# Three stretches of a causal attention reordered: the first queries' rotation, the output weights' split, the third norm's first transposes

## The chip, the cores and the metric

The kernel runs on one core of a Trainium2 chip. The metric is the device time of one execution in microseconds (us); lower is better. All positions below are counted from the start of the profiled execution's span.

## The reference

One layer over 512 rows of width 1024: x = x + cross_attention(norm(x)), x = x + causal_attention(norm(x)), x = x + feed_forward(norm(x)). The change touches the second part and the step into the third:

```python
q = x @ Wq + x @ q_A @ q_B          # 16 heads of 64; k and v have 4 heads
q, k = _rms_norm(q), _rms_norm(k)
q, k = _apply_rope(q, cos, sin), _apply_rope(k, cos, sin)
q = q * q_gain
attn = softmax(where(causal, q @ k.T * scale, -inf))
y = attn @ v
vn = v / maximum(sqrt(sum(v * v)), 1e-12)
y_out = y - sum(y * vn) * vn
out = y_out @ Wproj + y_out @ p_A @ p_B
x = x + out                          # then layernorm, router, experts
```

The feed-forward part has 16 routed experts (two for each row) and a shared one.

## The kernel before

Every large product is made in three passes of split operands (`matmul_3pass`, L32 to L34: hi by hi, hi by lo, lo by hi). The Scalar Engine (ACT) makes the hi half of an operand with a copy, VectorE (DVE) the lo half with a subtraction. Each engine has its own instruction list, written out by hand, and goes through it in order; semaphores join the lists. There is no planner, so the order in the source is the order in the queues.

`attention` holds both attentions. The cross attention (64 steps) ends near 900 us. Then the projections of the causal attention are made in twelve pieces, `ORDER`: four pieces hold keys and values of a block of 128 rows, eight hold half of a block's queries. Seven pieces (`AHEAD`) are made before the heads, and the other five are filled in between them.

For a piece, ACT copies the product out (`copy_piece`) and squares it by heads (`square_piece`), GpSimd (POOL) turns the mean squares into a factor (`root`, L651 and L654) and multiplies by the sines (`turn_by_sin`, L663), DVE multiplies by the factor (L1302) and by the cosines (L1305) in `turn_by_cos` and adds both parts in `rotate` (L1322). TensorE (PE) transposes the result (`turn_piece`, L846) and ACT copies it to `c_kT` or `c_qT` (`turned_piece`, L1097). Piece 4 is the first piece of queries. `unit_values` (L1330, L1332) squares and sums the values, POOL takes the square root (L711), and `unit_values_2` makes the unit vectors `vn`.

The heads go in 32 units of two heads, one a step, in 34 steps `st`. In each step PE makes the scores of unit st (L888), transposes the probabilities of unit st - 1 (L901) and multiplies those of unit st - 2 with the values (L917); DVE makes the maxima (`maxima`, L1347 and L1351), copies half of the transposed probabilities (`pt_dve`) and scales the result (`take_y`, L1369); ACT copies the other half (`pt_act`, L1104) and makes the exponentials (`exps`, L1113). Between these, PE does a third of a projection piece in each step (`fill`), from step 16 on a third of an output tile. `slot` places the transposes of query pieces and of finished rows (`turn_y`, L928; ACT `xt_hi`, L1060; DVE `xt_lo`, L1290) at half steps. POOL and DVE take the part along the value out of y: `times_value` (L681), `dot` (L1376), `part_along` (L687), `take_along` (L1383).

The weights of the output come as four pieces of 1 MB, w = 6 to 9, into two raw buffers. `weights_hi` (ACT, L1032) and `weights_lo` (DVE, L1222) split them in steps 10 to 18; the next load into a buffer waits for the split of the piece before it. After the steps PE makes the last transposes of rows (`turn_y`, 14 and 15), the transposes of the third norm's rows (`turn_xn`, L996) and output tiles 6 and 7 (`output`). `third_norm` (DVE, L96) makes those rows. Output tile 6 needs `xt_lo` of the last rows. The causal attention and this step end near 1128 us.

Of the kernel before, what the change touches and what calls it, by code (L numbers as in the profile page):

```python
# [427 lines left out]
def attention(nc, m, ins, resid, QT, K, V, raw, s_sb, PT, at, kv_loaded, ident, y_dram, ln, d, F, weff, weff_stored):  # L428
# [18 lines left out]
    with ExitStack() as stage:  # L447
# [60 lines left out]
        def w_piece(x, w):  # L508
            return x[:, (w // 2) % 2, 4 * (w % 2):4 * (w % 2) + 4, :]

        def w_raw(w):
            return raw[:, w % 2, :].rearrange("p (e n) -> p e n", n=W)
# [72 lines left out]
        with nc.Block() as block:  # L585
# [38 lines left out]
            def _(pool):  # L624
# [23 lines left out]
                def root(i):  # L648
                    n = heads(i)
                    pool.wait_ge(s["piece_out"], i + 1)  # L650
                    pool.tensor_scalar(ms[:, i % 3, 0:n], ms[:, i % 3, 0:n], 1.0 / HD, RMS_EPS,  # L651
                                       ALU.mult, ALU.add).then_inc(s["ms_done"], 1)
                    pool.wait_ge(s["ms_done"], i + 1)
                    pool.tensor_tensor(ms[:, i % 3, 0:n], ms[:, i % 3, 0:n],  # L654
                                       consts[:, 1:2].to_broadcast([P, n]), ALU.pow).then_inc(s["rms_done"], 1)

                def turn_by_sin(i):
                    n = heads(i)
                    pool.wait_ge(s["normed"], i + 1)
                    if i >= 2:  # L660
                        pool.wait_ge(s["rotated"], i - 1)
                    for k in range(2):
                        pool.tensor_tensor(half(sq[:, i % 2, :], i, k), half(piece_row(i), i, 1 - k),  # L663
                                           sin[:, tile_of(i), :].unsqueeze(1).to_broadcast([P, n, 32]),
                                           ALU.mult).then_inc(s["sin_done"], 1)
# [40 lines left out]
                for i in range(1, 5):  # L706
                    root(i)
                    turn_by_sin(i - 1)
                turn_by_sin(4)
                pool.wait_ge(s["vss"], 1)  # L710
                pool.tensor_tensor(vss[:, :], vss[:, :], consts[:, 2:3].to_broadcast([P, TB * HKV]),  # L711
                                   ALU.pow).then_inc(s["vnorm"], 1)
                root(5)
                turn_by_sin(5)
                root(6)
                turn_by_sin(6)
# [21 lines left out]
            def _(pe):  # L738
# [249 lines left out]
                def turn_xn(t):  # L988
                    pe.wait_ge(ln.xn_done, 2 * TB + t + 1)
                    for h in range(2):  # L990
                        n = 2 * t + h
                        if n >= 4:
                            pe.wait_ge(d["xt_lo_done"], n - 3)
                        for i in range(4):
                            e = 4 * h + i
                            mm = pe.transpose(xn_bank(n)[:, i * P:(i + 1) * P], F["xn"][:, t, e * P:(e + 1) * P],  # L996
                                              ident[:, :])
                        mm.then_inc(d["xt_ready"], 1)

                pe.wait_ge(s["y_done"], UNITS)  # L1000
                turn_y(4 * TB - 2)
                turn_y(4 * TB - 1)
                turn_xn(0)
                turn_xn(1)
                output(6, 0, DB)
                turn_xn(2)
# [7 lines left out]
            def _(act):  # L1014
# [11 lines left out]
                def weights_hi(w):  # L1026
                    raw_loaded(act, w % 2, w // 2 + (w >= 2))
                    if w < 4:
                        act.wait_ge(b["scores_ready"], STEPS if w >= 2 else SPLITS)
                    else:  # L1030
                        act.wait_ge(s["group_done"], w // 2 - 1)
                    act.activation(w_piece(K_hi, w), w_raw(w), ACT.Copy).then_inc(s["w_hi"], 1)  # L1032

                def step(base, u, known):
                    qb = u % TB
# [114 lines left out]
                for st in range(UNITS + 2):  # L1150
                    if st in TAKEN:
                        copy_piece(AHEAD + TAKEN.index(st))
                    slot(2 * st)
                    if 1 <= st <= UNITS:
                        pt_act(st - 1)
                    if st < UNITS:
                        exps(st)
                    if st == 0:
                        square_piece(6)
                    if st in TAKEN:  # L1160
                        square_piece(AHEAD + TAKEN.index(st))
                    slot(2 * st + 1)
                    for w, turn in ((6, 10), (7, 11), (8, 16), (9, 17)):
                        if st == turn:
                            weights_hi(w)

                def xn_hi(n):
                    act.wait_ge(d["xt_ready"], n + 1)
# [23 lines left out]
            def _(dve):  # L1192
# [27 lines left out]
                def weights_lo(w):  # L1220
                    dve.wait_ge(s["w_hi"], w + 1)
                    dve.tensor_tensor(w_piece(K_lo, w), w_raw(w), f32(w_piece(K_hi, w)),  # L1222
                                      ALU.subtract).then_inc(s["w_split"], 1)

                def add_x(t):

# [83 lines left out]
                def rotate(i):  # L1310
                    n = heads(i)
                    dve.wait_ge(s["cos_done"], i + 1)
                    dve.wait_ge(s["sin_done"], 2 * i + 2)
                    for k, op in enumerate((ALU.add, ALU.subtract)):
                        out = piece_row(i)
                        in0, in1 = half(cosp[:, i % 2, :], i, k), half(sq[:, i % 2, :], i, k)
                        if i < TB:
                            out = out.rearrange("p (h c d) -> p h c d", h=n, c=2)[:, :, :, k * 32:(k + 1) * 32]
                            in0, in1 = (x.unsqueeze(2).to_broadcast([P, n, 2, 32]) for x in (in0, in1))
                        else:  # L1320
                            out = out.rearrange("p (h d) -> p h d", d=HD)[:, :, k * 32:(k + 1) * 32]
                        ins_ = dve.tensor_tensor(out, in0, in1, op)  # L1322
                    ins_.then_inc(s["rotated"], 1)
# [4 lines left out]
                def unit_values():  # L1328
                    dve.wait_ge(s["piece_out"], TB)
                    dve.tensor_tensor(v_sq[:, :], v_flat, v_flat, ALU.mult).then_inc(s["v_step"], 1)  # L1330
                    dve.wait_ge(s["v_step"], 1)
                    dve.tensor_reduce(vss[:, :], v3(v_sq[:, :]), AX.X, ALU.add).then_inc(s["vss"], 1)  # L1332
# [66 lines left out]
                def third_norm(t):  # L1399
                    if t == 0:  # L1400
                        dve.wait_ge(s["w_split"], 10)
                    ln.norm(dve, 2, resid, F["xn"], mean_var, rstd, t)
# [43 lines left out]
                for i in range(1, 5):  # L1446
                    turn_by_cos(i)
                    rotate(i - 1)
                unit_values()
                rotate(4)  # L1450

                def slot(k):
                    for n, at_slot in ROWS_SLOTS.items():
# [3 lines left out]
                for st in range(UNITS + 2):  # L1457
                    if st >= 19 and st % 3 == 1:
                        add_out((st - 19) // 3)
                    slot(2 * st)  # L1460
                    if st < UNITS:
                        maxima(st)
                    if 1 <= st <= UNITS:
                        pt_dve(st - 1)
                        row_recip(st - 1)
                    if st >= 2:
                        take_y(st - 2)
                    if st >= 4 and st % 2 == 0:
                        dot((st - 4) // 2)
                    if st >= 5 and st % 2 == 1:  # L1470
                        take_along((st - 5) // 2)
                    slot(2 * st + 1)
                    if st == 0:
                        turn_by_cos(5)
                    if st == 1:
                        rotate(5)
                        unit_values_2()
                    if st == 2:
                        turn_by_cos(6)
                    if st == 3:  # L1480
                        rotate(6)
                    if st - 1 in TAKEN:
                        turn_by_cos(AHEAD + TAKEN.index(st - 1))
                    if st - 2 in TAKEN:
                        rotate(AHEAD + TAKEN.index(st - 2))
                    for w, turn in ((6, 10), (7, 12), (8, 16), (9, 18)):
                        if st == turn:
                            weights_lo(w)
                    if st >= 20 and st % 3 == 2:
                        half_stats((st - 20) // 6, (st - 20) // 3 % 2)  # L1490
                    if st in (27, 33):
                        third_norm((st - 27) // 6)
                dot(15)
                take_along(15)
                add_out(5)
                xt_lo(4 * TB - 2)
                xt_lo(4 * TB - 1)
# [1047 lines left out]
```

## Time and profile before

| | |
|---|---|
| runs of the kernel | 1451.96, 1452.84, 1455.63 us (median 1452.84) |
| profiled execution, its own time | 1451.73 us |
| its span | 1450.1 us |
| PE busy (matmuls) | 1408.3 us, 97% of the span |
| DVE busy | 845.6 us, 58% |
| ACT busy | 530.3 us, 37% |
| POOL busy | 202.8 us, 14% |
| median from issue to landing of a load of output weights | 4.7 us |

A row of the timeline has the start, the duration (from the first start to the last end, for several instructions in one row), engine, line and operation, the tiles written and read, and the count; in brackets stands the idle time before it and what ended it. The granted clock is that of TensorE, 1.00 for 2.4 GHz and 0.50 for 1.2 GHz. Matmul durations overlap each other, so the distance of two starts says more than one duration.

### The profile page before, as it was taken

Reading aid. Unit: us, or ns where it says so; the run is one execution under the profiler, and the core shown is the slowest. Engines: PE = TensorE matmul, PEld = TensorE weight load, DVE = VectorE, ACT = ScalarE, POOL = GpSimd, SP = SyncE. Lnnn points to the kernel's source line nnn. Section 1 sums busy time; section 2 is a strip of 40 time slices with the busy share of each in tenths; the row PEclk is TensorE's granted clock in tenths of the full one; section 3 lists DMA queues with packets and bytes.
Section 4 is the critical chain, followed back from the end, with each engine's and each line's share of the span. In section 5 each row is a group of like instructions: output and inputs, shape, how many; then the busy total and the mean of one; then the engine's idle time right before and its main releaser. Section 6 shows DMA issues by size and latency. Waiting matters only on the chain. (4 is left out here: it accounts for less than half of the span.)

```text
span 1450.1 us, 18196 instructions
## 1 busy us (share of the span) xinstructions
PE 1408.3 (97%) x6676; PEld 1151.2 (79%) x6676; DVE 845.6 (58%) x1232; ACT 530.3 (37%) x947; POOL 202.8 (14%) x264
## 2 busy tenths in 40 slices
PE   7999999999999999999999999899999899998998
PEld 5878788888888888888888888776778788887786
DVE  5554455555555455455554557678765676676655
ACT  3222322332223322223222223556432435665561
POOL 3000100000000000000000000455311022122132
PEclk9999999999999999999999999999999999999999
DMA  7453643333333333333333322201100566886766
GB/s 251 152 202 118 247 176 118 116 109 108 123 123 111 113 108 115 131 108 116 108 112 131 108 98 77 107 1 59 34 1 1 175 210 228 299 294 222 266 224 218
DMA packets 43487, 203.64 MB, mean 140 GB/s; under 512 B 5233, under 2 KB 5297, under 8 KB 31985
## 3 DMA queue, kind: packets, MB, share of 16 engines
q1 hardware_dynamic: 30016, 152.32, 30.1%
q0 software_dynamic: 9568, 36.35, 7.7%
q10 hardware_dynamic: 3840, 14.16, 2.5%
q8 instruction: 37, 0.61, 0.2%
q14 instruction: 26, 0.20, 0.0%
HBM read 182.36 MB, written 20.45 MB: 140 GB/s over the span
## 5 line engine op out<-in xcount | busy, mean ns | idle before, releaser
L32 PE MATMUL banks<-V_hi,b_PT_hi 128*128 128x512 f32 x512 | 205.6, 401 | 0.0
L1024 ACT ACTIVATE b_PT_hi<-banks 128x512 fp32r<-128x512 f32 x64 | 38.3, 599 | 446.9 <-PE banks L757 446.9
L32 PE MATMUL banks<-K_hi,QT_hi 128*128 128x512 f32 x512 | 199.3, 389 | 2.5 <-PEq L157 2.5
L34 PE MATMUL banks<-V_hi,b_PT_lo 128*128 128x512 f32 x512 | 200.2, 391 | 0.0
L33 PE MATMUL banks<-V_lo,b_PT_hi 128*128 128x512 f32 x512 | 199.6, 390 | 0.0
L34 PE MATMUL banks<-K_hi,QT_lo 128*128 128x512 f32 x512 | 199.4, 389 | 0.0
L33 PE MATMUL banks<-K_lo,QT_hi 128*128 128x512 f32 x512 | 199.2, 389 | 0.0
L1247 DVE TENSOR_TENSOR b_scores<-banks,b_scores 128x512 f32<-128x512 f32 x64 | 44.2, 691 | 202.0 <-PE banks L34 202.0
L642 POOL DMA_DIRECT2D b_scores<-mask x60 | 32.2, 537 | 639.2 <-PE banks L757 621.4
L2176 DVE TENSOR_TENSOR e_lo<-e_raw,e_hi 128x1024 fp32r<-128x1024 f32 x80 | 95.2, 1231 | 38.4 <-ACT e_hi L2012 37.3
L32 PEld LDWEIGHTS banks<-K_hi,QT_hi 128*128 128x128 f32 x512 | 96.1, 188 | 22.8 <-issue 2.9
L34 PEld LDWEIGHTS banks<-V_hi,b_PT_lo 128*128 128x128 f32 x512 | 96.1, 188 | 21.0
L34 PEld LDWEIGHTS banks<-K_hi,QT_lo 128*128 128x128 f32 x512 | 96.1, 188 | 20.0
L33 PEld LDWEIGHTS banks<-K_lo,QT_hi 128*128 128x128 f32 x512 | 96.1, 188 | 19.9
L33 PEld LDWEIGHTS banks<-V_lo,b_PT_hi 128*128 128x128 f32 x512 | 96.4, 188 | 18.5
L32 PEld LDWEIGHTS banks<-V_hi,b_PT_hi 128*128 128x128 f32 x512 | 96.2, 188 | 18.0
L1267 DVE TENSOR_TENSOR V_lo<-raw,V_hi 128x2048 fp32r<-128x2048 f32 x30 | 68.8, 2292 | 64.4 <-ACT V_hi L1048 64.4
L1267 DVE TENSOR_TENSOR K_lo<-raw,K_hi 128x2048 fp32r<-128x2048 f32 x30 | 68.8, 2293 | 61.8 <-ACT K_hi L1048 61.8
L2012 ACT ACTIVATE e_hi<-e_raw 128x1024 fp32r<-128x1024 f32 x80 | 81.4, 1060 | 23.0 <-DMA e_raw<-w_down 16.1
L1204 DVE SCALAR_TENSOR_TENSOR resid<-resid,b_alpha,banks 128x1024 f32<-128x1024 f32 x60 | 76.5, 1275 | 6.8 <-PE banks L34 6.8
L32 PE MATMUL banks<-K_hi,V_hi 128*128 128x512 f32 x160 | 68.2, 427 | 0.8 <-ACT c_piece L1069 0.8
L34 PE MATMUL banks<-K_hi,V_lo 128*128 128x512 f32 x160 | 64.0, 400 | 0.0
(327 smaller groups left out, 2752.4 us busy)
## 6 DMA issues: line engine op xcount, KB each, us to landing
raw<-kv SPq DMA_DIRECT2D x60, 1024.0 KB, 4.7
e_raw<-w_up SPq DMA_DIRECT2D x40, 512.0 KB, 5.0
e_raw<-w_down SPq DMA_DIRECT2D x40, 512.0 KB, 5.9
b_scores<-mask POOLq DMA_DIRECT2D x64, 256.0 KB, 2.9
d_s_raw<-shared_w SPq DMA_DIRECT2D x32, 512.0 KB, 4.9
raw<-xattn_w SPq DMA_DIRECT2D x11, 1024.0 KB, 4.9
y_dram<-c_zeros ACTq DMA_DIRECT2D x1, 6656.0 KB, 28.0
raw<-attn_w SPq DMA_DIRECT2D x6, 1024.0 KB, 4.7
```

What stands on the lines that cost most here:

```text
L32: pe.matmul(out, lhs_hi, rhs_hi, start=first, stop=False)
L33: pe.matmul(out, lhs_hi, rhs_lo, start=False, stop=False)
L34: return pe.matmul(out, lhs_lo, rhs_hi, start=False, stop=last)
L642: pool.dma_start(s_sb[:, u, :], ins["mask"][it * 4 + u]).then_inc(mask_loaded[u], 16)
L1024: act.activation(PT_hi[:, u % 2, :], T_ps[:, u % 2, :], ACT.Copy).then_inc(b["pt_hi"], 1)
L1204: op = dve.scalar_tensor_tensor(resid[:, qb, :], resid[:, qb, :], alpha[:, qb:qb + 1], O_ps(u), ALU.mult, ALU.add)
L1247: dve.tensor_tensor(s_sb[:, u % 4, :], S_ps[:, u % 2, :], s_sb[:, u % 4, :], ALU.add).then_inc(b["masked"], 1)
L1267: dve.tensor_tensor(split_tile(False, u), raw_tile(u), f32(split_tile(True, u)), ALU.subtract).then_inc(b["kv_split"], 1)
L2012: act.activation(e_hi[:, first + j, :], e_raw[:, j, :], ACT.Copy).then_inc(s["e_hi"], 1)
L2176: dve.tensor_tensor(e_lo[:, first + j, :], e_raw[:, j, :], f32(e_hi[:, first + j, :]), ALU.subtract).then_inc(s["e_split"], 1)
```

## The change

Three edits. First, DVE rotates piece 4 before `unit_values()`, and POOL takes `root(5)` before the root of the values' squares. Second, each of the output weight pieces is split in two halves of 128 x 1024, one a step, on ACT in steps 10 to 13 and 15 to 18 and on DVE in steps 11 to 14 and 16 to 19. Third, PE transposes the third norm's first rows (`turn_xn(0)`) before the last rows of heads, and DVE makes the norm of rows 1 after the last `take_along` and not in step 33.

```diff
--- before.py
+++ after.py
@@ -707,10 +707,10 @@
                     root(i)
                     turn_by_sin(i - 1)
                 turn_by_sin(4)
+                root(5)
                 pool.wait_ge(s["vss"], 1)
                 pool.tensor_tensor(vss[:, :], vss[:, :], consts[:, 2:3].to_broadcast([P, TB * HKV]),
                                    ALU.pow).then_inc(s["vnorm"], 1)
-                root(5)
                 turn_by_sin(5)
                 root(6)
                 turn_by_sin(6)
@@ -997,10 +997,10 @@
                                               ident[:, :])
                         mm.then_inc(d["xt_ready"], 1)
 
+                turn_xn(0)
                 pe.wait_ge(s["y_done"], UNITS)
                 turn_y(4 * TB - 2)
                 turn_y(4 * TB - 1)
-                turn_xn(0)
                 turn_xn(1)
                 output(6, 0, DB)
                 turn_xn(2)
@@ -1030,6 +1030,15 @@
                     else:
                         act.wait_ge(s["group_done"], w // 2 - 1)
                     act.activation(w_piece(K_hi, w), w_raw(w), ACT.Copy).then_inc(s["w_hi"], 1)
+
+                def output_weights_hi(w, part):
+
+                    if part == 0:
+                        raw_loaded(act, w % 2, w // 2 + 1)
+                        act.wait_ge(s["group_done"], w // 2 - 1)
+                    rows = slice(2 * part, 2 * part + 2)
+                    act.activation(w_piece(K_hi, w)[:, rows, :], w_raw(w)[:, rows, :],
+                                   ACT.Copy).then_inc(s["w_hi"], 1)
 
                 def step(base, u, known):
                     qb = u % TB
@@ -1160,9 +1169,9 @@
                     if st in TAKEN:
                         square_piece(AHEAD + TAKEN.index(st))
                     slot(2 * st + 1)
-                    for w, turn in ((6, 10), (7, 11), (8, 16), (9, 17)):
-                        if st == turn:
-                            weights_hi(w)
+                    for w, turn in ((6, 10), (7, 12), (8, 15), (9, 17)):
+                        if turn <= st < turn + 2:
+                            output_weights_hi(w, st - turn)
 
                 def xn_hi(n):
                     act.wait_ge(d["xt_ready"], n + 1)
@@ -1221,6 +1230,14 @@
                     dve.wait_ge(s["w_hi"], w + 1)
                     dve.tensor_tensor(w_piece(K_lo, w), w_raw(w), f32(w_piece(K_hi, w)),
                                       ALU.subtract).then_inc(s["w_split"], 1)
+
+                def output_weights_lo(w, part):
+                    rows = slice(2 * part, 2 * part + 2)
+                    dve.wait_ge(s["w_hi"], 2 * w - 6 + part + 1)
+                    op = dve.tensor_tensor(w_piece(K_lo, w)[:, rows, :], w_raw(w)[:, rows, :],
+                                           f32(w_piece(K_hi, w))[:, rows, :], ALU.subtract)
+                    if part:
+                        op.then_inc(s["w_split"], 1)
 
                 def add_x(t):
 
@@ -1446,8 +1463,8 @@
                 for i in range(1, 5):
                     turn_by_cos(i)
                     rotate(i - 1)
+                rotate(4)
                 unit_values()
-                rotate(4)
 
                 def slot(k):
                     for n, at_slot in ROWS_SLOTS.items():
@@ -1483,15 +1500,16 @@
                         turn_by_cos(AHEAD + TAKEN.index(st - 1))
                     if st - 2 in TAKEN:
                         rotate(AHEAD + TAKEN.index(st - 2))
-                    for w, turn in ((6, 10), (7, 12), (8, 16), (9, 18)):
-                        if st == turn:
-                            weights_lo(w)
+                    for w, turn in ((6, 11), (7, 13), (8, 16), (9, 18)):
+                        if turn <= st < turn + 2:
+                            output_weights_lo(w, st - turn)
                     if st >= 20 and st % 3 == 2:
                         half_stats((st - 20) // 6, (st - 20) // 3 % 2)
-                    if st in (27, 33):
-                        third_norm((st - 27) // 6)
+                    if st == 27:
+                        third_norm(0)
                 dot(15)
                 take_along(15)
+                third_norm(1)
                 add_out(5)
                 xt_lo(4 * TB - 2)
                 xt_lo(4 * TB - 1)
```

## Rows read from the trace of the kernel before

**Rows 1.** windows of 50 us: PE, PEld, DVE, ACT, POOL busy, clock, DMA
```profile
900.00:950.00 50.00, 45.97 (x206) 36.39 (x205) 32.84 (x48) 26.32 (x110) 22.60 (x27) 0.93 0.30 106
```

**Rows 2.** windows of 1 us, PE: length, busy, granted clock, DMA share, GB/s
```profile
990.00:991.00 1.00, 0.24 (x3) 0.96 0.50 205
...
994.00:995.00 1.00, 1.00 (x7) 0.83 0.35 49
```

**Rows 3.** PE's waits from 980 to 1025: us in total, times, longest
```profile
PE banks L901 <- ACT c_probs L1113: 1.2, 2, 0.8
PE banks L917 <- ACT c_qT L1097: 0.8, 1, 0.8
PE banks L32 <- ACT c_piece L1069: 0.8, 1, 0.8
PE banks L917 <- DVE V_lo L1290: 0.6, 2, 0.3
```

**Rows 4.** timeline, DVE, 920 to 962: start, us, line, tiles, count, idle before
```profile
936.45 1.21 DVE L1330 TENSOR_TENSOR c_v_sq<-c_v 128x1024 f32<-128x1024 f32 x1
...
938.83 0.77 DVE L1322 TENSOR_TENSOR c_piece<-c_cosp,c_sq 128x256 f32<-128x256 f32 x2
...
948.02 0.74 DVE L1322 TENSOR_TENSOR c_piece<-c_cosp,c_sq 128x256 f32<-128x256 f32 x2
...
951.38 0.27 DVE L1369 TENSOR_TENSOR c_y<-banks,c_recip 128x128 f32<-128x128 f32 x1
```

**Rows 5.** timeline, POOL, 920 to 962
```profile
934.13 2.11 POOL L663 TENSOR_TENSOR c_sq<-c_piece,c_sin 128x256 f32<-128x256 f32 x2 [0.63 <-DVE c_piece L1302]
938.99 3.00 POOL L711 TENSOR_TENSOR c_vss<-c_vss,c_consts 128x16 f32<-128x16 f32 x1 [2.75 <-DVE c_vss L1332]
...
942.37 1.63 POOL L654 TENSOR_TENSOR c_ms<-c_ms,c_consts 128x8 f32<-128x8 f32 x1
945.01 1.92 POOL L663 TENSOR_TENSOR c_sq<-c_piece,c_sin 128x256 f32<-128x256 f32 x2 [1.01 <-DVE c_piece L1302]
```

**Rows 6.** timeline, PE, 925 to 965
```profile
939.65 1.09 PE L846 MATMUL banks<-ident,c_piece 128*128 128x128 f32 x4 [2.42 <-DVE c_piece L1322]
941.43 0.80 PE L888 MATMUL banks<-c_kT,c_qT 64*128 64x128 f32 x4 [0.69 <-ACT c_qT L1097]
```

**Rows 7.** timeline, ACT, 920 to 962
```profile
937.77 0.59 ACT L1069 ACTIVATE c_piece<-banks 128x512 f32<-128x512 f32 x1
```

**Rows 8.** timelines of DVE, POOL and PE, 975 to 1030
```profile
983.75 2.82 DVE L1222 TENSOR_TENSOR K_lo<-raw,K_hi 128x2048 fp32r<-128x2048 f32 x1
...
983.18 3.98 POOL L663 TENSOR_TENSOR c_sq<-c_piece,c_sin 128x256 f32<-128x256 f32 x2 [0.63 <-DVE c_piece L1302]
...
995.27 0.70 PE L888 MATMUL banks<-c_kT,c_qT 64*128 64x256 f32 x4
```

**Rows 9.** groups by form, 900 to 1130: busy us, mean ns, idle before
```profile
L1411 DVE TENSOR_TENSOR d_s_lo<-d_s_raw,d_s_hi 128x1024 fp32r<-128x1024 f32 x2 | 2.4, 1217 | 0.0
```

**Rows 10.** timeline, PE, 1086 to 1135
```profile
1105.62 1.06 PE L928 MATMUL banks<-ident,c_y 128*128 128x128 f32 x8 [1.99 <-DVE c_y L1383]
1106.52 3.17 PE L996 MATMUL banks<-ident,e_raw 128*128 128x128 f32 x16
1109.34 0.77 PE L32 MATMUL banks<-K_hi,V_hi 128*128 128x512 f32 x1
...
1110.34 0.42 PE L34 MATMUL banks<-K_hi,V_lo 128*128 128x512 f32 x1
```

**Rows 11.** timelines of DVE and POOL, 1086 to 1135
```profile
1102.77 1.23 DVE L96 TENSOR_SCALAR e_raw<-resid,c_mean_var,c_rstd 128x1024 f32<-128x1024 f32 x1
1103.92 0.41 DVE L1376 TENSOR_REDUCE c_dots<-c_along 128x4 f32<-128x256 f32 x1
...
1111.31 0.81 DVE L96 TENSOR_SCALAR e_raw<-resid,c_mean_var,c_rstd 128x1024 f32<-128x1024 f32 x1
...
1102.60 0.85 POOL L681 TENSOR_TENSOR c_along<-c_y,c_vn 128x256 f32<-128x256 f32 x1 [2.93 <-DVE c_y L1369]
```

## The prediction

> **What bounds the kernel now.** I read the page first. TensorE (PE) is busy 97% of the span, so a change can only pay where PE waits or where its clock falls. The windows of 50 us show where that is: in 900 to 950, where the causal attention begins, PE is busy 46.0 us and its granted clock is 0.93 [rows 1]. The windows of 1 us show what a fall costs. The clock was 0.96 of full in 990 to 991, 0.50 in the three windows after it, and 0.83 in 994 to 995 [rows 2]: it fell from the 2.4 GHz to the 1.2 GHz level for 0.08 + 3 + 0.34 = 3.4 us, right after PE had waited twice for 0.8 us [rows 3]. At half speed that is 1.7 us lost, the price I use for one fall below. Then the chain of waits and the timeline give the three places the diff touches. I count times in the old trace from the span's start, and take three savings A, B and C.
>
> **A, the first queries' rotation.** VectorE (DVE) begins `unit_values()`, the squares of the values and their sums, at 936.45 and comes to `rotate(4)` at 938.8 [rows 4]. PE waits for exactly this: its transposes `turn_piece(4)` start at 939.65 after 2.42 us of idleness, and the first scores at 941.43, after 0.69 us more [rows 6]. New order: `rotate(4)` runs 936.5 to 937.2, its sines being ready at 934.1 + 2.1 = 936.2 [rows 5]. `turn_piece(4)` follows `turn_piece(3)` without a gap, at 937.3. Scalar Engine (ACT) must then copy the result to `c_qT`, but its copy of piece 6 stands ahead and ends at 938.3 [rows 7]; the copy of about 0.6 us ends at 938.9. So the first scores move from 941.4 to 938.9, 2.5 us.
>
> What is late next? The values' squares are now behind the rotation, so they end at 939.6 instead of 938.8, and GpSimd (POOL) takes its root of them (3.0 us) from 939.7 to 942.7. It does `root(5)` first, which costs 1.9 us (its longer instruction 1.63) [rows 5] but falls into time in which POOL idled for 2.7 us. Before, the sines of piece 5 stood behind both roots and started at 945.0; now they start at 942.7 and end at 944.6. `rotate(5)` then runs at 944.7 instead of 948.0, 3.3 us earlier [rows 4]; it was queued behind the second maxima, which come early enough now. Behind it, in DVE's order, stand `unit_values_2()`, the third maxima and `take_y(0)`, which ended at 951.65 [rows 4] and now end at 948.3. PE's `turn_piece(5)` waits for that. So A is worth 3.3 us by then. PE, at full clock, would be there 1.8 us before it and waits. If the low clock of before comes back (the first scores took 0.80 us in it [rows 6]), some 3 us remain all the same, since PE then arrives late and DVE's chain is hidden. Low bound 1.5 (the wait of 1.8 us brings one fall behind it), high bound 4.3 (DVE not in the way). The number of instructions doesn't change.
>
> The Trainium skill (SBUF — State Buffer, section Who interferes with whom) says that VectorE operations with two SBUF inputs and GpSimd operations exclude each other for a whole instruction. The trace agrees in part: a subtraction took 2.82 us where POOL's pair of multiplications took 3.98 at the same time [rows 8]. By that rule the squares would wait for `root(5)` until 938.2 and A would be 2.3 instead of 3.3.
>
> **B, the output weights by halves.** Before, DVE subtracts a whole weight piece at the end of step 10: it starts at 983.75 and takes 2.82 us, so the maxima of step 11, ready earlier, come late; ACT's exponentials come late, and PE's transposes wait 0.8 us for them. ACT then converts a whole weight piece of its own before the copy of piece 10, and PE waits 0.8 us for that copy [rows 3, 8]. These two waits and the fall that followed are 0.8 + 0.8 + 1.7 = 3.3 us. In the new order step 10 has no DVE half, and steps 11 and 12 have one each. A half is about 1.22 us on DVE, by the row of the same subtraction at that size [rows 9]; two are 2.44 where one whole beside POOL took 2.82 [rows 8], so the split itself costs some tenths of a us in all, on engines with slack in the other steps. I followed DVE: maxima(11) at 983.9, the half ends about 988.6, maxima(12) ends at 989.7 and its exponentials at 990.7. PE comes for them at 992.6. So the scores of step 13 start at 992.0 instead of 995.27 [rows 8], which is 3.3 us.
>
> Then it gives a part back. In steps 13 and 14 the halves meet the cosines and the rotation of piece 10. DVE has about 5.3 us of work in each, and PE 4.1 to 4.9. The rows of heads, `xt_lo(8)` and `xt_lo(9)`, come 0.2 us later each than PE, and the waits for them (0.6 in all [rows 3]) grow to 1.0. A half on ACT at the end of step 15 delays nothing that PE waits for: the copy of piece 10's transposes, for which PE waits 0.8 us [rows 3], stands ahead of it. In step 18 PE's last transposes of a piece wait about 0.9 us for `take_y`, as maxima(18) stand behind a half. The wait of 0.4 us in step 17 for the exponentials goes, as before it stood behind a whole subtraction. Net 3.3 - 0.4 + 0.4 - 0.5 = 2.8 us. Bounds 0.5 (a fall in steps 15 to 17, with 0.6 lost to longer waits) and 3.7. The loads are no matter: a raw buffer is free one or two steps later, and its 1 MB lands 4.7 us after the issue, with over 4 us left before the step that reads it.
>
> **C, the third norm.** Before, PE has nothing from 1103.6 until its transposes at 1105.62, 1.99 us [rows 10]: `take_along(15)` waits for POOL, which waits for `dot(15)` at 1103.92, and that stood behind a norm of 1.23 us [rows 11]. New: `turn_xn(0)` fills PE at 1103.6 with 0.8 us of transposes (16 took 3.17 us at half clock, so 8 take 0.8 [rows 10]). `dot(15)` needs POOL's product, which was there at 1102.60 + 0.85 = 1103.45 [rows 11], so the chain is 0.4 us earlier and `turn_y` starts at 1105.2 and ends at 1106.0. The norm of row 1 runs 1105.0 to 1105.8, since POOL is idle then (0.81 us in that state, 1.23 beside POOL [rows 11]). `turn_xn(1)` ends at 1106.8. `add_out(5)` (0.7) and `xt_lo(14)` (0.7) follow the norm and end at 1107.1, which releases output(6). It started at 1109.34, and its first two products ran at the low clock, so that the third began at 1110.34 where it now begins at 1107.64 [rows 10]. C is 2.7 us. If the clock falls all the same, it is 1.0; if the norm takes 1.23, it is 2.3. Everything behind output(6) hangs on it, up to the end of the block at 1128.
>
> **Sum.** 3.3 + 2.8 + 2.7 = 8.8 us with no new fall. PE's idle stretches are shorter but not gone. The wait of 1.8 us at 946.5 and two of about 0.8 in steps 15 and 16 look like those after which the clock fell. I take half of one fall, 0.8 us: 8.0 us. The profiled execution took 1451.73 (span 1450.1), which gives 1443.7; the median of the runs is 1.1 above it, so 1444.8.
>
> **Rivals.**
> - *The waits move and the clock falls in the new ones* (0.26). For it speaks that PE then waits on DVE in the steps named. With two or three falls the gain is 8.8 - 3.4 to 8.8 - 5.1, so 1447.5 to 1449. Against: the wait of 0.8 us for `c_qT` [rows 3] had no fall behind it. The Trainium skill (TensorE: Matmul & The Clock Gate, section The HAM clock gate) says that the gate judges by a free-running measure, so that the same wait may or may not be followed by a fall; the trace agrees, since waits of 0.8 us went both ways.
> - *The time is taken back* (0.10). The feed-forward part streams expert weights, and where loads set its pace an earlier start might not end earlier. Against: those loads are issued only after routing, which follows output(7), so they move along. Two thirds lost would give 1449 to 1452.
> - *DVE becomes the bound and keeps PE at 1.2 GHz* (0.04). One mechanism: the halves in steps 13 to 19 stall PE in each step and the clock stays low through all of them. Those are some 30 us, of which half, 15 us, would be added, less the 6 of A and C: 1462. It decides from about 9 us of low clock net of B on. Against: before, the waits of steps 13 to 17 with whole pieces had no fall.
> - *More than forecast* (0.08): a fall elsewhere goes, or A reaches its high bound: 1441 to 1442.
> - *The forecast*, all three waits gone with at most one fall: gain 7 to 9.5, 1443.3 to 1446 (0.52).
>
> **The numbers.** Faster and slower are counted from 0.3% (4.4 us), about what a measurement here can tell. Faster: the forecast, the better case, and two thirds of the first rival, 0.77, of which I keep 0.76 as the runs of before spread over 3.7 us. Slower is the third rival, 0.04; no change the rest, 0.20. Eight in ten: 1441.5 to 1450.
>
> **What would show it.** A: no idle over 1 us before `turn_piece(4)`, first scores near 938.9, a new wait near 946.5. B: step 13's scores 3.3 us earlier against step 10's, at full clock. C: `turn_xn(0)` right behind the last output block and output(6) 2.2 us earlier against it. I am wrong if the squares or `take_y(0)` come later than worked out, or if the clock is 0.50 in more stretches than before.

## The result, and the profile after

The changed kernel takes 1447.79 us (median of 16 runs, 1444.25 to 1452.07) against 1452.86 us of before (16 runs). The ratio (time over that of before) is 0.9965, with a 95% interval of 0.9955 to 0.9974: 5.1 us or 0.35% faster, between 3.8 and 6.5. The forecast was 8.0 us. The time lies in its range, and its direction was right; the size was 1.6 times too large. The profiled execution's span is 1447.4 us.

First edit. PE's timeline of the changed kernel, from 936 us (start, duration, line, tiles, count, idle time before and what ended it):

```profile
939.07 0.66 PE L846 MATMUL banks<-ident,c_piece 128*128 128x128 f32 x4 [0.30 <-DVE c_piece L1339]
940.43 0.49 PE L888 MATMUL banks<-c_kT,c_qT 64*128 64x128 f32 x4 [0.70 <-ACT c_qT L1106]
...
950.00 0.66 PE L846 MATMUL banks<-ident,c_piece 128*128 128x128 f32 x4 [0.43 <-DVE c_y L1386]
```

DVE and POOL in the same stretch of the same kernel:

```profile
938.24 0.78 DVE L1339 TENSOR_TENSOR c_piece<-c_cosp,c_sq 128x256 f32<-128x256 f32 x2 [0.18 <-issue]
938.94 1.21 DVE L1347 TENSOR_TENSOR c_v_sq<-c_v 128x1024 f32<-128x1024 f32 x1
...
949.68 0.27 DVE L1386 TENSOR_TENSOR c_y<-banks,c_recip 128x128 f32<-128x128 f32 x1
```

```profile
938.20 1.63 POOL L654 TENSOR_TENSOR c_ms<-c_ms,c_consts 128x8 f32<-128x8 f32 x1
941.49 2.89 POOL L712 TENSOR_TENSOR c_vss<-c_vss,c_consts 128x16 f32<-128x16 f32 x1 [1.65 <-DVE c_vss L1349]
944.34 1.41 POOL L663 TENSOR_TENSOR c_sq<-c_piece,c_sin 128x256 f32<-128x256 f32 x2
```

This execution entered the causal attention 1.53 us later than that of before (its first key transposes stand at 929.55, those of before at 928.02), for a reason outside the change: its clock was at half level for one stretch from 156 to 159.4 us, behind an idle 2.50 us of PE that the profile of before has too. Eight of this study's 14 profiles have that stretch, and their first key transposes stand at 929.2 to 929.8; in the six without it they stand at 927.4 to 928.6. So places are compared against the first key transposes. The idle 2.42 us of [rows 6] is now 0.30, and the first scores stand 10.88 us behind the first key transposes instead of 13.41.

Second edit. PE, DVE and POOL at steps 13 and 14, and the windows of 1 us behind them (length, PE busy, granted clock, DMA share, GB/s):

```profile
990.19 0.70 PE L888 MATMUL banks<-c_kT,c_qT 64*128 64x256 f32 x4
...
995.00 0.70 PE L888 MATMUL banks<-c_kT,c_qT 64*128 64x256 f32 x4
...
997.67 1.08 PE L917 MATMUL banks<-c_v,c_PT 128*128 128x64 f32 x8 [1.37 <-DVE V_lo L1307]
```

```profile
995.17 1.75 DVE L1237 TENSOR_TENSOR K_lo<-raw,K_hi 128x1024 fp32r<-128x1024 f32 x1
996.84 0.68 DVE L1307 TENSOR_TENSOR V_lo<-banks,V_hi 128x512 fp32r<-128x512 f32 x1
```

```profile
994.61 2.89 POOL L663 TENSOR_TENSOR c_sq<-c_piece,c_sin 128x256 f32<-128x256 f32 x2 [0.83 <-DVE c_piece L1319]
```

```profile
998.00:999.00 1.00, 1.00 (x9) 1.00 0.00 0
999.00:1000.00 1.00, 1.00 (x4) 0.50 0.00 0
...
1002.00:1003.00 1.00, 1.00 (x8) 0.80 0.61 90
```

The two waits of 0.8 us of [rows 3], for the probabilities of step 11 and the copy of piece 10, are gone: step 13 stands 13.06 us behind step 10, before 16.45. But in step 14 PE waits 1.37 us for `xt_lo(8)`, which stands on DVE behind a half that took 1.75 us beside POOL's sines, and then the clock goes to 1.2 GHz for 3.4 us. Step 15 comes 12.41 us behind step 13, before 9.56.

Third edit. PE and DVE at the end of the steps:

```profile
1101.27 1.04 PE L996 MATMUL banks<-ident,e_raw 128*128 128x128 f32 x8
1103.00 1.06 PE L928 MATMUL banks<-ident,c_y 128*128 128x128 f32 x8 [0.70 <-DVE c_y L1400]
1103.90 1.04 PE L996 MATMUL banks<-ident,e_raw 128*128 128x128 f32 x8
1105.04 0.50 PE L32 MATMUL banks<-K_hi,V_hi 128*128 128x512 f32 x1
```

```profile
1102.43 0.42 DVE L1400 TENSOR_TENSOR c_y<-c_y,c_along 128x256 f32<-128x256 f32 x1 [0.73 <-POOL c_along L687]
1102.77 0.81 DVE L96 TENSOR_SCALAR e_raw<-resid,c_mean_var,c_rstd 128x1024 f32<-128x1024 f32 x1
```

`turn_xn(0)` fills PE, 0.70 us of the 1.99 us of idleness [rows 10] remains, the norm takes 0.81 us, and output(6) starts 17.55 us behind step 31, before 19.65.

The table takes differences of PE's start times in the timelines: first key transposes (k), scores of steps 3, 10, 13, 15, 20 and 31, first product of output(6), first product after the attention (e), end of the span. It is for all profiles of this study.

```
kernel            k to 3  3-10  10-13  13-15  15-20  20-31  31-out6  out6-e  e-end
before             25.43  25.37  16.45   9.56  25.05  59.81   19.65   19.00  321.8
before_again       25.19  25.39  14.91   9.56  25.06  59.78   20.16   18.51  323.4
after              22.19  25.39  13.06  12.41  25.08  59.81   17.55   18.54  323.8
all_again          21.81  25.39  13.05  10.81  25.14  59.81   17.55   18.51  329.1
a_alone            21.79  25.38  16.52   9.55  25.06  59.81   18.50   18.49  326.5
b_alone            25.29  25.39  13.05  10.81  25.12  59.81   18.50   18.54  324.3
c_alone            25.23  25.39  16.50   9.58  25.05  59.81   17.55   18.51  324.1
a_and_c            22.15  25.39  14.93   9.55  25.05  59.81   17.55   18.51  323.9
steps_13_14_free   21.80  25.39  13.05   9.74  25.13  59.82   17.55   18.56  323.7
vn_later           20.17  26.11  13.05  12.39  25.13  59.81   17.55   18.54  324.8
both               21.71  26.12  13.05   9.75  25.13  59.82   17.55   18.56  325.5
pool_order_back    26.73  25.82  13.05  10.82  25.13  59.77   17.55   18.51  326.3
norm_in_step_33    21.81  25.39  13.06  10.81  25.12  59.78   17.97   18.54  325.5
turn_xn_after      21.80  25.39  13.05  10.82  25.11  59.78   18.08   18.49  327.4
```

Up to e, the columns repeat to 0.1 us from kernel to kernel except where a stretch at half clock lies in them or an edit acts. That makes this table a sharper measure than the times, whose 95% intervals are 3 to 6 us wide.

### The profile page after: what moved, and what is told of

It is laid out like the page before. It is cut to its first block and busy times, and to the rows that moved or that the text cites. A ratio compares the mean times of both kernels' runs of the same rounds, so it can differ in the third digit from the quotient of the medians.

```text
span 1447.4 us, 18204 instructions
## 1 busy us (share of the span) xinstructions
PE 1411.5 (98%) x6676; PEld 1153.5 (80%) x6676; DVE 847.0 (59%) x1236; ACT 529.8 (37%) x951; POOL 198.6 (14%) x264
```

## The experiments

In this part, a "fall" is a stretch at half clock. Where only a ratio and a saving are given, the saving is worked out from the ratio. Theory 1: each edit is worth what its place in the trace shows, and the split of the weights fell short of its term. Theory 2: the feed-forward part takes a share back. Rival on the split: its step was right, and the fall behind step 14 was chance.

**a_alone.** The first edit alone, on the kernel before:

```diff
-                unit_values()
                 rotate(4)
+                unit_values()
```

(and POOL's `root(5)` ahead of the root of the squares).

> Only the first edit (rotation of piece 4 before the squares of the values, root(5) before their root). Theory 1 (each edit is worth what its place in the trace shows; split of the weights is what fell short): the scores of step 3 stand 3.2 us earlier against the last key projections, and the time is 3 us (0.2%) below before, ratio 0.998. Theory 2 (the feed-forward part takes back a share of any saving): the same 3.2 us at step 3, but only about 2 us in the time, ratio 0.9985, with the span from the end of the attention to the end longer than before's 322 us in profile after profile.

Measured: 1449.91 us, before 1452.94; ratio 0.9976 (0.9965 to 0.9987), 3.5 us. Step 3 is 3.6 us earlier than in the first profile of before and 3.4 than in the second. The clock kept its full level here, and PE then shows the wait that the prediction gave as 1.8 us. PE's timeline of a_alone:

```profile
948.26 0.66 PE L846 MATMUL banks<-ident,c_piece 128*128 128x128 f32 x4 [1.61 <-DVE c_y L1369]
```

In the changed kernel's first profile the clock was low from 941.0 to 944.4, PE came later and waited 0.43, and step 3 was 3.2 us earlier than in the first profile of before. So the term holds at either level. Theory 1 holds in the attention and in the time; theory 2's 2 us are at the edge of the interval (1.9 to 5.1). The part behind the attention took 326.5 us, as theory 2 wanted, but it varies from profile to profile of all kernels (see the end of the next section).

**b_alone.** The second edit alone: `output_weights_hi` and `output_weights_lo` with the steps of the diff, the rest as before.

> Only the second edit (output weights by halves). Theory 1: the scores of step 13 are 3.3 us earlier against those of step 10, then PE waits over 1 us for the lo half of the first row transposes (xt_lo(8)) in step 14; what is left by step 15 is 0 to 1 us, with a clock fall behind that wait, or 2 without; ratio 0.9985 to 1.0. Rival (the clock fall at step 14 of the changed kernel's profile was chance and the split is worth the 2.8 us of the prediction): step 15 is 2 to 3 us earlier, ratio 0.998.

Measured: 1452.15 us against 1452.94; ratio 0.9991 (0.9979 to 1.0003), in which no gain is shown. Step 13 comes as early as in the full change (13.05 us), and step 15 is 10.81 us behind it although the clock did not fall there. PE's waits in 925 to 1130 of b_alone:

```profile
PE banks L917 <- DVE V_lo L1307: 1.7, 2, 1.4
```

From step 10 to 15 that is 23.9 us, against 26.0 in the first profile of before, which has a fall there, and 24.5 in the second, which has none. Theory 1 holds: the wait for `xt_lo(8)` comes without a fall too, and the 2.8 us of the prediction are not reached.

**c_alone.** The third edit alone.

> Only the third edit (turn_xn(0) before the last rows of heads, norm of row 1 after take_along(15)). Theory 1: from the last output block before it to the first product of output(6) 2.5 us less than before, and 2.5 us off the time, ratio 0.9983. Theory 2 (feed-forward takes back): 2.5 us at output(6) but 1.5 us in the time, ratio 0.999.

Measured: 1451.62 us; ratio 0.9990 (0.9978 to 1.0002), 1.5 us. Step 31 to output(6) is 17.55 us. Against the first profile of before that is 2.1 us, plus 0.5 in the next column. But a_alone and b_alone, which have the old order there, show 18.50: the same wait of 2.0 us, without the fall behind it. PE's waits of a_alone, and below of c_alone:

```profile
PE banks L928 <- DVE c_y L1383: 2.0, 1, 2.0
...
PE banks L928 <- DVE c_y L1383: 0.7, 1, 0.7
```

The third edit saves 0.95 us from step 31 to output(6) in every profile, and the rest only where the clock would have fallen. The 2.5 us that theory 1 expected there were missed for that reason. The interval in the time (from 0.3 us slower to 3.2 faster) doesn't tell the theories apart.

**a_and_c.** First and third edit, weights whole as before.

> First and third edit, weights split in whole pieces as before. Theory 1: 3.2 + 2.5 = 5.7 us, about the time of the full change or at most 1 us above it, ratio 0.996. Rival (the split carries 2.8 us): 2 to 3 us slower than the full change, ratio 0.998.

Measured: 1447.71 us; ratio 0.9966 (0.9951 to 0.9980), the same as the full change. In this profile both waits of 0.8 us stand at steps 11 and 12,

```profile
PE banks L901 <- ACT c_probs L1113: 1.2, 2, 0.8
...
PE banks L32 <- ACT c_piece L1069: 0.8, 1, 0.8
```

and the clock didn't fall behind them (windows of 4 us: length, PE busy, granted clock):

```profile
990.00:994.00 4.00, 4.00 (x27) 1.00 0.25 43
```

So it takes 14.93 us from step 10 to 13, where the first profile of before has 16.45. Theory 1 holds. From step 10 to 20 it takes 49.53 us; all_again, with the split and without a fall, takes 49.00. So the split saves 0.5 us where neither falls. With a fall in each, it is 51.06 (before) against 50.55 (after), 0.5 again. How often each falls is another matter: with whole pieces three of five profiles have the fall near 990 (before, a_alone and c_alone, the three with 16.5 in the column 10-13), with the halves of the change two of seven have the one behind step 14 (after and vn_later, the two with 12.4 in 13-15). That may be worth another 0.5 us on the average of many executions, an estimate from these counts at 1.5 us a fall; they are too few to show it.

**steps_13_14_free.** The full change with the halves in other steps. On DVE:

```diff
-                    for w, turn in ((6, 11), (7, 13), (8, 16), (9, 18)):
-                        if turn <= st < turn + 2:
-                            output_weights_lo(w, st - turn)
+                    for w, part, turn in ((6, 0, 11), (6, 1, 12), (7, 0, 12), (7, 1, 15),
+                                          (8, 0, 16), (8, 1, 17), (9, 0, 18), (9, 1, 19)):
+                        if st == turn:
+                            output_weights_lo(w, part)
```

and on ACT the halves of pieces 6 and 7 in steps 10, 10, 11 and 13.

> The full change with other places for the halves: DVE's second half of piece 6 and first half of piece 7 in step 12, the second of piece 7 in step 15, none in steps 13 and 14. Theory 1 (the split fell short because its halves meet the cosines and rotation of piece 10 in steps 13 and 14): step 13 stays 13.0 to 13.3 us behind step 10 and step 15 comes 9.5 to 9.8 us behind step 13, against 12.4 in the full change; the wait for xt_lo(8) is 0.3 us again; 1.5 to 2.5 us below the full change. Rival (the fall behind step 14 was chance, the halves harmless): step 15 as before too, but no gain in time over the full change beyond 0.5 us.

Measured: 1445.79 us against 1453.14 of before; ratio 0.9949 (0.9929 to 0.9968), 7.4 us, from six runs. Step 13 keeps its place (13.05 us) and step 15 is 9.74 us behind it, 1.1 us less than in all_again. PE's waits from 925 to 1130 of steps_13_14_free, and DVE's two halves in step 12, beside each other:

```profile
PE banks L917 <- DVE V_lo L1308: 0.6, 2, 0.3
```

```profile
988.27 2.77 DVE L1238 TENSOR_TENSOR K_lo<-raw,K_hi 128x1024 fp32r<-128x1024 f32 x2
```

The waits for `xt_lo` are back at the 0.6 us of [rows 3]. Halves moved on ACT too, but in the changed kernel's first profile `xt_lo(8)` followed on DVE right behind the half, without idle time in which it would have waited for ACT. So the halves of DVE in steps 13 and 14 were the cause of the wait. From step 10 to 20 it takes 47.92 us, 1.1 less than the full change and 1.6 less than whole pieces, all without a fall. The medians differ from all_again by 3.2 us, but the intervals of the two ratios overlap; the 1.1 us are what the trace shows, and a fall that can follow the longer wait comes on top.

**all_again.** The full change unaltered.

> The full change once more, unaltered, for its second profile. Theory 1 (the wait for xt_lo(8) is structural, the falls of the clock are partly chance): the waits of PE in the attention are the same within 0.1 us, that of 1.4 us among them, while the stretches at half clock stand elsewhere or differ in number. Rival (the falls are structural): the same stretches as in the first profile.

Measured: 1449.02 us; ratio 0.9968 (0.9955 to 0.9981). PE's waits from 925 to 1130, and the windows behind steps 13 and 14:

```profile
PE banks L846 <- DVE c_y L1386: 2.8, 3, 1.6
...
PE banks L917 <- DVE V_lo L1307: 1.7, 2, 1.4
```

```profile
994.00:998.00 4.00, 2.63 (x20) 1.00 0.00 0
998.00:1002.00 4.00, 4.00 (x26) 1.00 0.02 4
```

The wait of 1.4 us is there as in the first profile, the fall behind it is not. So the wait belongs to the program, and the fall does not follow from it alone: the instructions are the same in both. The one wait that differs is that for `take_y` (1.6 instead of 0.43), since no fall stood at 941 either.

**before_again.** The kernel before, unaltered.

> The kernel before, unaltered, for a second profile. Theory 1 (its waits are structural, its falls of the clock are chance): waits of 2.4, 2.0, 0.8 and 0.8 us as in the first profile, but stretches at half clock elsewhere or in another number; end of the attention to end of the span more than the 321.8 us of the first profile, like the 324 to 329 of the others. Rival: the same stretches, 322 us.

Measured: 1451.07 us in its one run. Its clock by windows of 4 us (length, PE busy, granted clock):

```profile
942.00:946.00 4.00, 4.00 (x12) 0.50 0.00 0
...
990.00:994.00 4.00, 3.78 (x21) 1.00 0.01 2
1102.00:1106.00 4.00, 2.74 (x14) 0.69 0.01 4
```

PE's waits are those of the first profile: 2.4 us before the first queries' transposes, 2.0 before the last rows, 0.8 and 0.8 at steps 11 and 12. But there is no fall at 990, where [rows 2] show one, and the fall behind the wait of 2.0 us comes from 1103 and not from 1107. The part behind the attention took 323.4 us, more than the 321.8 of the first profile as theory 1 wanted, and at the low end of the others. One fall repeats: that behind the rotation (between 939 and 948), some 6.8 us long, stands in all four profiles with the old order of the first edit; with the new order one of 3.4 us stands there in four of ten.

**vn_later.** The full change, with the unit vectors one step later:

```diff
                         rotate(5)
-                        unit_values_2()
                     if st == 2:
+                        unit_values_2()
                         turn_by_cos(6)
```

> The full change, with unit_values_2() behind take_y(0) in step 2 instead of ahead of the third maxima in step 1. Theory 1 (what limits the first edit is DVE's queue ahead of take_y(0)): where the clock stays at full level PE's wait of 1.6 us before turn_piece(5) goes and step 3's scores come 20.2 to 20.6 us behind the first key transposes; with a fall at 940, 21.8 to 22.2. Time 0 to 1.5 us below the full change. Rival (POOL's root of the values' squares is the limit): the wait stays at 1 us or more.

Measured: 1447.17 us; ratio 0.9960 (0.9942 to 0.9978). Step 3 stands 20.17 us behind the first key transposes, 1.6 us earlier than in all_again, and the wait of 1.6 us before `turn_piece(5)` is gone. PE's waits from 925 to 1130 of vn_later, where all_again has 2.8, 3, 1.6:

```profile
PE banks L846 <- DVE c_y L1386: 1.2, 2, 0.7
```

The queue on DVE ahead of `take_y(0)` is the limit. But 0.7 us come back by step 10 (26.11 instead of 25.39). In the time it can't be told from the full change.

**both.** The two alterations together.

> The full change with both alterations (halves out of steps 13 and 14, unit_values_2() behind take_y(0)). Theory 1: the sum of the two, 1.5 to 4 us below the full change, about 1445. Rival: within 0.5 us of the full change.

Measured: 1447.29 us; ratio 0.9953 (0.9936 to 0.9971), within 0.0004 of steps_13_14_free, with a median 1.5 us above it. The two gains did not add up to anything that the time shows. A fall stood at 939 to 943, so the shift of the unit vectors brought nothing at step 3 (21.71 us), and it costs 0.7 us behind it again (26.12).

**pool_order_back.** The full change with POOL's old order (the root of the squares ahead of `root(5)`).

> The full change with POOL's old order: the root of the values' squares ahead of root(5). Theory 1 (the first edit needs both halves, since the squares now come later): the first scores stay 10.9 us behind the first key transposes, but root(5) ends near 944.7, the rotation of piece 5 comes 1.9 us or more later and step 3's scores come 24 us behind, against 21.8 or 22.2 in the full change; about 2 us slower than it. Rival (POOL has slack): no difference.

Measured: 1454.47 us; ratio 1.0007 (0.9990 to 1.0024), some 6 us slower than the full change, more than either theory said. Its POOL and PE timelines:

```profile
944.65 1.63 POOL L654 TENSOR_TENSOR c_ms<-c_ms,c_consts 128x8 f32<-128x8 f32 x1
947.29 1.90 POOL L663 TENSOR_TENSOR c_sq<-c_piece,c_sin 128x256 f32<-128x256 f32 x2 [1.01 <-DVE c_piece L1319]
```

```profile
949.64 0.44 PE L901 MATMUL banks<-ident,c_probs 128*128 128x128 f32 x2 [1.68 <-ACT c_probs L1122]
...
953.03 1.12 PE L846 MATMUL banks<-ident,c_piece 128*128 128x128 f32 x4 [1.63 <-DVE c_y L1386]
```

The first scores stand where the full change has them (10.89 us), but the sines come 3 us later, DVE waits in order for `rotate(5)` with the second step's maxima behind it, and PE waits 1.68 and 1.63 us within some 5 us. The clock went low from 940.6 to 944.0 and again from 950.9 for 6.8 us. Step 3 comes 26.7 us behind the first key transposes, later than before the change, and later than the 24 us expected. I had left out that a second wait comes up and that the clock falls behind both.

**norm_in_step_33.** The full change with `third_norm(1)` back in step 33.

> The full change with the norm of row 1 back in step 33, turn_xn(0) still ahead. Theory 1: dot(15) waits for the norm as before, 0.4 us later; the wait of 0.7 us becomes 1.1 us, but the lo halves of the last rows come without the norm ahead of them; step 31 to output(6) 17.3 to 18.0 us against 17.55. Rival (the norm's place carries the third edit): 18.5 us.

Measured: 1448.29 us; ratio 0.9966 (0.9953 to 0.9979). Step 31 to output(6) is 17.97 us, 0.42 more, and PE's wait for the last rows is 1.1 us instead of 0.7, as theory 1 said:

```profile
PE banks L928 <- DVE c_y L1400: 1.1, 1, 1.1
```

**turn_xn_after.** The full change with `turn_xn(0)` back behind the last rows.

> The full change with turn_xn(0) back behind the last rows of heads, the norm still late. Theory 1 (both parts are needed): PE idles 1.5 us ahead of the last rows, and step 31 to output(6) is 18.2 to 18.6 us without a fall (19.2 to 19.7 with one) against 17.55. Rival: 17.6 us.

Measured: 1449.33 us; ratio 0.9973 (0.9961 to 0.9985). Step 31 to output(6) is 18.08 us, 0.53 more and a little less than the 18.2 to 18.6 expected, with a wait of 1.6 us:

```profile
PE banks L928 <- DVE c_y L1400: 1.6, 1, 1.6
```

So the 0.95 us are the sum of the two parts, 0.42 and 0.53.

## Why the prediction was right in direction and too large in size

- **A, 3.3 us: right.** In the columns it is 3.0 to 3.6 us, by which profiles are compared, in the time of a_alone 3.5. The first scores came 2.5 us earlier as worked out, the roots ran 938.2 to 944.4 in place (less 1.5 us of offset, 936.7 to 942.8), and the wait of 1.8 us showed as 1.61 where the clock stayed up. The Trainium skill's rule on shared ports (SBUF — State Buffer, section Who interferes with whom) would have delayed the squares until `root(5)` ended. They started at 938.94 with the root drawn from 938.20 to 939.83 (the profile's spans of POOL are rough), and took 1.21 us as ever, so for this pair the measurement decides against the rule. It holds better for the long operations: the half at 995.17 and POOL's sines beside it took 1.75 and 2.89 us, and 2.89 us together; alone they took 1.21 (985.57 in the same profile) and 1.92 (945.01 in [rows 5]), which is 3.13 one behind the other.

```profile
985.57 1.21 DVE L1237 TENSOR_TENSOR K_lo<-raw,K_hi 128x1024 fp32r<-128x1024 f32 x1
```

- **B, "net 2.8 us": the failed step.** The first half of it, 3.3 us at step 13, came out as 3.4. Two things in it were wrong. "The waits for `xt_lo` grow to 1.0" from 0.6: they measured 1.7. I had put the half of step 13 at 1.2 us; it runs beside POOL's sines and takes 1.75, which is 0.5 of the 0.7 us that were missing. From step 13 to 15 the halves cost 1.3 us in every profile without a fall there (10.81 against 9.55 us), where the sum had 0.4. And "0.8 + 0.8 + 1.7" counted the fall at 990 as if it came each time. It is there in a_alone and c_alone, and missing in the profiles of before_again and a_and_c, which have the same waits. Without it the split brings 1.9 us at step 13 and loses 1.4 by step 20, and 0.5 us is left. With a fall on either side it is 0.5 too.
- **C, 2.7 us: the mechanism right, the term mis-sized.** Each place on PE and DVE that the prediction named came out within 0.2 us of the forecast, once the 2.2 us by which everything there stood earlier are taken off. But 1.2 us of the saving, and 0.5 in the next stretch, were the fall of [rows 10] and are absent in two profiles with the old order. What each execution gains is 0.95 us. Behind that wait of 2.0 us the clock fell in two of four profiles; behind the shorter ones of 0.7 to 1.6 us in the ten other profiles, in none.
- **The rival "the waits move and the clock falls in the new ones"** is in part what happened: a wait moved to step 14 and a fall followed it in one of two profiles of the changed kernel. The measured 1447.8 lies in the range given to this rival (1447.5 to 1449) and outside that of the forecast (1443.3 to 1446). That the stated range holds it as well owes more to its width than to the sum. The rival of the split as DVE's bound was not seen: no stretch stayed low beyond 3.4 us there.
- **Sum.** What is gone whether the clock falls or not: A about 3.3, B 0.5, C 1.0, together 4.8 us; the times say 5.1 (3.8 to 6.5). Fewer falls behind the waits of B and C would add 1.3 us on the average (an estimate from the counts above, 0.5 and half of 1.7), so the close agreement of 4.8 and 5.1 may be luck.

What stays open is the feed-forward part. From the first product after the attention to the end it took 321.8 and 323.4 us in two profiles of before and 323.7 to 329.1 in the twelve others, whose instructions there are the same. The time at half clock in it differs from profile to profile. Counted in lengths of 3.4 us and without the one at the very end, there is one in the first profile of before and three in the second, and two to six in the others. The part took 321.8 us with one, 323.4 to 324.3 with two to four, 324.8 to 326.5 with five, and 327.4 and 329.1 with six. Two profiles of before are too few to say whether an earlier start makes them more frequent; the times leave room for about 1 us of it, and no run separates it.

## What to carry to other kernels

A wait read from one profile belongs to the program, and repeated here to 0.1 us as long as the clock was the same ahead of it; a fall of the clock behind it need not repeat, so count it in a sum only where several profiles show it. An operation split and spread over steps must be placed by what each step already holds, and priced beside the engine that runs with it: the same halves in steps 12 and 15 instead of 13 and 14 were worth 1.1 us more. When one engine's order is turned, the engine that feeds its next item must be turned too; with POOL's old order the first edit lost all its gain and more.

## What the runs showed of the hardware

Away from the end of the span, the clock stood at half level for stretches of 3.4 us or twice that in all 14 profiles. Such a stretch came behind two waits of 0.8 us, behind one of 1.4 us and behind one of 2.0 us, and behind the same waits in one profile and not in another of the same instructions. In all_again one starts near 1153 us though PE was busy without a break from 1135 on. A power on POOL took 1.63 to 1.69 us for 8 values in each of the 128 partitions and 2.89 to 3.00 us for 16.
